# Four MetaFormer layers on one core: the wide stages' down products as three 64-column products, their eviction as a copy

## The chip, the cores and the metric

One core of one Trainium2 chip runs the whole program in one launch. The metric is the device time in microseconds (us), given as the median of several runs. TensorE's clock has two levels in the records, 1.2 and 2.4 GHz; the granted clock is given as a share of the upper one.

## The reference, cut to what matters

Sixteen images of 64 channels and 24 x 24 pixels go through four layers. Each layer normalizes, applies a small convolution-like mixer (a covariance gate, dynamic ReLU, a Haar gate, a 3x3 depthwise convolution), normalizes again and runs a mixture of eight experts on the 9216 tokens. Layers 0 and 1 run every expert on every token. Layers 2 and 3, the wide stages, send each token to its two best experts and compute

```python
h = silu(x @ w1[e].T) * (x @ w3[e].T)     # 64 -> 682
y = h @ w2[e].T                           # 682 -> 64
```

weighted by the router. The kernel computes in float16 pairs: a number is split into a high and a low half, and the three products high x high, high x low and low x high are added in float32. For the down projection, h is the pair in the tile `hl` (high half first, low half behind it), and w2 is the pair in the tiles `dW`, where each expert has 64 high columns and then 64 low columns.

## The kernel before, in words

The five engines each have one long, unrolled stream of instructions; semaphores tie them. A wide stage (`moe`) works on 80 tiles of 256 token rows, sorted by expert, in 20 rounds of four tiles (UNROLL). A tile belongs to one expert, known only at run time, so each expert's weights are addressed through a register of TensorE: `words`, `chosen` and `bases` (L1817 to L1830) decode the expert's number and multiply it by the width of one expert's columns.

A tile has three groups g. For each group TensorE runs, in this order written out by hand in `body23` (L1866):

- `up23` (L1832): eight products of 256 columns, gate and up, each for two blocks c of 114 hidden units and for the high and the low half of the weights (L1843 and L1844). Every one of these takes its weight block from another tile (gA, gB, uA, uB) at the offset in the register.
- `down23` (L1849) of the tile before: for each of two blocks c and two blocks u of 128 tokens, one product of the high half of h with 128 columns of weights, the 64 high and 64 low ones (L1860), and one of the low half of h with the 64 high columns (L1862). So a group has eight products, a tile 24, and the two stages 1920 of each line. The results for one u lie in 128 columns of an output bank: columns 0 to 63 hold high x high plus low x high, columns 64 to 127 hold high x low.

Once for each tile there are also two transposes of the next rows (`turn_rows`, L1814) and the decoding of the next expert (`settle`, L1823, called from L1846).

ScalarE takes the gate through Silu (L885) and rounds h to its high half (L893). VectorE multiplies (L1391), makes the low half (L1395) and, once for each tile, two tiles behind TensorE, adds the two 64-column halves out of the bank into the output row buffer (`evict`, L1372, the reduction at L1381). GpSimd then scatters each row buffer to memory (L675). The output banks are PB[4] and PB[5], used in turn.

The first two layers (`dense`) have a down step (L1785) that already runs three products of 64 columns into one place, from weights at a fixed address.

Of the kernel before, what the change touches and what calls it, by code (L numbers as in the profile page):

```python
# [21 lines left out]
ALU = mybir.AluOpType  # L22
ACT = mybir.ActivationFunctionType
AX = mybir.AxisListType
ds = bass.ds

B, C, HW = 16, 64, 24
PIX = HW * HW
P = 128
# [8 lines left out]
SUB = ROWS // P  # L38
# [16 lines left out]
CH = 114  # L55
# [171 lines left out]
def program(nc, I, out):  # L227
    ctx = ExitStack()
    with ctx:
        def sb(name, shape, dt=FP32):  # L230
            return ctx.enter_context(nc.sbuf_tensor(name, shape, dt))

        def sem(name):
            return ctx.enter_context(nc.semaphore(name))
# [79 lines left out]
        hl = [sb(f"hl{i}", [P, 4 * ROWS], FP16) for i in range(SPLIT)]  # L314
# [20 lines left out]
        PB = [ctx.enter_context(nc.psum_tensor(f"bank{i}", [P, 512], FP32)) for i in range(8)]  # L335
# [31 lines left out]
        s = {n: sem(n) for n in names}  # L367
# [23 lines left out]
        def group_base(l):  # L391

            return (l - SPARSE) * TILES * G

        def unit_base(l, h):
            return n_of(l, h) * NUNIT
# [29 lines left out]
        def tile_base(l):  # L426
            return (l - SPARSE) * TILES

        def ring(t):

            return t % YRING, 16 * SUB * (t // YRING)
# [10 lines left out]
        def inner():  # L442

            todo, begin, over = [LN1 + k / 4 for k in range(8)], JOIN_AT * G, JOIN_OVER * G
            return [-1] * begin + [todo[min(len(todo), -(-(v + 1) * len(todo) // over)) - 1] for v in range(NSLOT - begin)]
# [3 lines left out]
        def split_base(l):  # L449

            return (l - SPARSE) * TILES * SPLIT

        def hold(k, g):

            return prod[g]

        def wait_from(eng, semaphore, value):

            if not isinstance(value, int) or value > 0:
                eng.wait_ge(semaphore, value)  # L460
# [492 lines left out]
        def _(v):  # L953
# [414 lines left out]
            def moe(l, aside):  # L1368
                tb, gb = tile_base(l), group_base(l)
                plan = inner()  # L1370

                def evict(i, k):  # L1372

                    t = i * UNROLL + (tb + k)
                    v.wait_ge(s["y_grp"], i * (UNROLL * G) + (gb + (k + 1) * G))

                    r, before = ring(t)
                    wait_from(v, y_st[r], before)
                    y = ysb[r][:, :].rearrange("p (u c) -> p u c", u=SUB)
                    src = PB[4 + k % 2][:, 0:SUB * 2 * C].rearrange("p (u s c) -> p u c s", u=SUB, s=2)  # L1380
                    ins = v.tensor_reduce(y, src, AX.X, ALU.add)  # L1381
                    ins.then_inc(s["y_done"], 1)

                sb_ = split_base(l)

                def product(i, k, g):
                    q = k * G + g
                    p = hold(k, g)[0:CH, :]
                    v.wait_ge(s["s_ready"], i * (UNROLL * G) + (gb + q + 1))
                    v.wait_ge(s["h_ps"], i * (UNROLL * G) + (gb + q + 1))  # L1390
                    v.tensor_tensor(p, PB[2 + q % 2][0:CH, :], p, ALU.mult).then_inc(s["prod_ready"], 1)  # L1391

                def low(i, k, g):
                    v.wait_ge(s["hi_ready"], i * (UNROLL * SPLIT) + (sb_ + k * SPLIT + g + 1))
                    v.tensor_tensor(hl[g][0:CH, 2 * ROWS:4 * ROWS], hold(k, g)[0:CH, :], hl[g][0:CH, 0:2 * ROWS], ALU.subtract  # L1395
                                    ).then_inc(s["hp_ready"], 1)

                def body23(i, first=False):

                    for k in range(UNROLL):  # L1400
                        for g in range(G):
                            product(i, k, g)
                            if g > 0:
                                low(i, k, g - 1)
                            elif k > 0:
                                low(i, k - 1, G - 1)
                            elif not first:
                                low(i - 1, UNROLL - 1, G - 1)
                            if g == 0 and k >= 2:
                                evict(i, k - 2)  # L1410
                            elif g == 0 and not first:
                                evict(i - 1, k + UNROLL - 2)
                            if aside is not None:
                                aside.upto(plan[(i * UNROLL + k) * G + g])
                if l == SPARSE:
                    v.wait_ge(s["added"], unit_base(SPARSE, 0))
                body23(0, first=True)
                for i in range(1, LOOPS - 1):
                    body23(i)
                body23(LOOPS - 1)  # L1420
                low(LOOPS - 1, UNROLL - 1, G - 1)
                evict(LOOPS - 1, UNROLL - 2)
                evict(LOOPS - 1, UNROLL - 1)
                if aside is not None:
                    aside.upto(LAST)
# [111 lines left out]
        def _(pe):  # L1537
# [264 lines left out]
            def moe(l):  # L1802
# [46 lines left out]
                def down23(i, k, g):  # L1849


                    pe.wait_ge(s["hp_ready"], i * (UNROLL * SPLIT) + (split_base(l) + k * SPLIT + g + 1))
                    y = PB[4 + k % 2]
                    at = ds(bases[i * UNROLL + k, 1], 2 * C)
                    for c in range(2):
                        w = dW[2 * g + c][:, at]
                        for u in range(SUB):
                            col = c * ROWS + u * P
                            o = u * 2 * C
                            pe.matmul(y[:, o:o + 2 * C], hl[g][0:CH, col:col + P], w,  # L1860
                                      start=(g == 0 and c == 0 and u == 0), stop=False, skip_group_check=True)
                            ins = pe.matmul(y[:, o:o + C], hl[g][0:CH, 2 * ROWS + col:2 * ROWS + col + P],  # L1862
                                            w[:, 0:C], start=False, stop=(g == G - 1 and c == 1), skip_group_check=True)
                    ins.then_inc(s["y_grp"], 1)

                def body23(i, first=False, last=False):  # L1866

                    for k in range(UNROLL):
                        if not (last and k + 2 >= UNROLL):
                            turn_rows(i, k, 2)  # L1870
                        for g in range(g_):
                            up23(i, k, g, not (last and k == UNROLL - 1))
                            if k > 0:
                                down23(i, k - 1, g)
                            elif not first:
                                down23(i - 1, UNROLL - 1, g)
                            if g == 0 and k == 2 and not last:
                                fetch(i + 1)
                    if last:
                        for g in range(g_):  # L1880
                            down23(i, UNROLL - 1, g)
# [68 lines left out]
```

## Time and profile before

| | us |
|---|---|
| median of 3 runs | 2027.19 (2026.78 to 2030.93) |
| profiled execution, its own time | 2032.62 |
| span of the profile, first to last instruction | 2030.8 |
| mean granted clock of TensorE in the span | 0.826 |

The profile gives, for one execution, each engine's instructions with start and duration. PE is TensorE's products, PEld its weight loads, which overlap the products; PEldq is what TensorE's own instruction queue executes beside them (register arithmetic, semaphore waits), and these are not counted as busy. A product's duration includes its way through the array, so the distance from one start to the next says what it costs in a row of products. An idle time put down to "issue" is one in which the engine waited for nothing that the profile shows.

### The profile page before, as it was taken

Reading aid. Unit: us, or ns where it says so; the run is one execution under the profiler, and the core shown is the slowest. Engines: PE = TensorE matmul, PEld = TensorE weight load, DVE = VectorE, ACT = ScalarE, POOL = GpSimd, SP = SyncE. Lnnn points to the kernel's source line nnn. Section 1 sums busy time; section 2 is a strip of 40 time slices with the busy share of each in tenths; the row PEclk is TensorE's granted clock in tenths of the full one; section 3 lists DMA queues with packets and bytes.
Section 4 is the critical chain, followed back from the end, with each engine's and each line's share of the span. In section 5 each row is a group of like instructions: output and inputs, shape, how many; then the busy total and the mean of one; then the engine's idle time right before and its main releaser. Section 6 shows DMA issues by size and latency. Waiting matters only on the chain.

```text
span 2030.8 us, 47407 instructions
## 1 busy us (share of the span) xinstructions
PE 1452.7 (72%) x16020; PEld 1087.5 (54%) x16020; DVE 1687.7 (83%) x2922; ACT 1281.8 (63%) x2367; POOL 938.8 (46%) x899
## 2 busy tenths in 40 slices
PE   3648899526777776688349999995331449999994
PEld 2545444515333343344248888884221248888884
DVE  5676888697778858888669999999868769999998
ACT  1026899212999967499228888886320138888883
POOL 1003778100233311167027777656216757777653
PEclk9756999575999967699559999997655669999997
DMA  8000000000000100000001111210300011111212
GB/s 324 1 0 29 2 29 2 0 0 0 29 29 29 57 1 1 1 22 27 8 15 42 42 41 42 81 32 8 130 0 18 22 32 43 42 41 41 79 33 99
DMA packets 49470, 74.98 MB, mean 37 GB/s; under 512 B 13636, under 2 KB 34235, under 8 KB 46590
## 3 DMA queue, kind: packets, MB, share of 16 engines
q1 hardware_dynamic: 28354, 42.26, 6.5%
q0 software_dynamic: 20896, 29.73, 4.3%
q8 instruction: 146, 2.39, 0.5%
q14 instruction: 74, 0.61, 0.1%
HBM read 39.88 MB, written 33.08 MB: 36 GB/s over the span
## 4 chain that ended last, share of the span: by engine, by line
PE 37%; DVE 17%; issue 4%; ACT 2%; DMA 0%; POOLq 0%; POOL 0%; DVEq 0%; SPq 0%; ACTq 0%
PE bank L1843 13%; PE bank L1844 11%; PE bank L1860 5%; PE bank L1862 3%; DVE tmp L1181 2%; DVE x L1483 2%; PE bank L1715 1%; PE bank L1564 1%; PE bank L1814 1%; DVE xn L1003 1%; DVE st L1001 1%; DVE tmp L1154 1%; ACT hl L868 1%; DVE xn L1022 1%; DVE st L1002 1%
## 5 line engine op out<-in xcount | busy, mean ns | idle before, releaser
L689 POOL TENSOR_TENSOR x<-x,ysb 128x256 f32<-128x256 f32 x248 | 232.8, 939 | 620.9 <-DVE ysb L1489 603.6
L636 POOL DMA_INDIRECT rows<-rowsb,pos x288 | 306.7, 1065 | 205.7 <-DVE pos L1310 119.2
L868 ACT ACTIVATE hb<-bank,bias_sb 128x512 f32<-128x512 f32 x432 | 315.2, 730 | 85.0 <-issue 42.0
L675 POOL DMA_INDIRECT y<-w,ids x256 | 283.8, 1109 | 136.2 <-DVE w L1381 71.5
L1843 PE MATMUL bank<-xT,uA_ 128*114 128x256 f16 x960 | 258.0, 285 | 5.3
L1843 PE MATMUL bank<-xT,gA_ 128*114 128x256 f16 x960 | 251.2, 286 | 5.9 <-issue 3.6
L1844 PE MATMUL bank<-xT,uB_ 128*114 128x256 f16 x960 | 253.3, 278 | 0.0
L1391 DVE TENSOR_TENSOR act<-bank,act 114x512 f32<-114x512 f32 x320 | 219.8, 687 | 36.0 <-PE bank L1844 16.6
L885 ACT ACTIVATE act<-bank 114x512 f32<-114x512 f32 x320 | 191.2, 597 | 81.6 <-PE bank L1844 67.2
L1844 PE MATMUL bank<-xT,gB_ 128*114 128x256 f16 x960 | 242.3, 275 | 0.0
L1860 PE MATMUL bank<-dW_,hl 114*128 x1920 | 229.1, 220 | 3.1 <-DVE hl L1395 3.1
L1395 DVE TENSOR_TENSOR hl<-act,hl 114x512 f16<-114x512 f32 x320 | 218.3, 682 | 0.0
L1862 PE MATMUL bank<-dW_,hl 114*128 x1920 | 214.4, 192 | 0.0
L1472 DVE TENSOR_TENSOR hl<-hb,hl 128x512 f16<-128x512 f32 x216 | 165.6, 766 | 49.2 <-ACT hl L868 39.9
L1472 DVE TENSOR_TENSOR act<-hb,act 128x512 f16<-128x512 f32 x216 | 164.4, 761 | 43.8 <-ACT act L868 34.0
L893 ACT ACTIVATE hl<-act 114x512 f16<-114x512 f32 x320 | 199.1, 622 | 1.9 <-DVE act L1391 1.7
L1769 PE MATMUL bank<-rowsb,w 128*128 128x512 f16 x432 | 177.3, 410 | 4.2 <-DMA land<-land 3.5
L1770 PE MATMUL bank<-rowsb,w 128*128 128x512 f16 x432 | 177.2, 410 | 0.0
L1564 PE MATMUL bank<-K,xn 128*128 128x128 f32 x144 | 38.1, 409 | 193.2 <-DVE xn L1022 169.2
L1860 PEld LDWEIGHTS bank<-dW_,hl 114*128 114x128 f16 x1920 | 170.3, 97 | 7.1 <-issue 4.5
L1862 PEld LDWEIGHTS bank<-dW_,hl 114*128 114x128 f16 x1920 | 170.2, 98 | 0.0
L868 ACT ACTIVATE act<-bank,bias_sb 128x512 f16<-128x512 f32 x216 | 158.1, 732 | 0.0
(389 smaller groups left out, 3461.8 us busy)
## 6 DMA issues: line engine op xcount, KB each, us to landing
stage<-up SPq DMA_DIRECT2D x8, 1368.0 KB, 7.1
xs<-rows SPq DMA_DIRECT2D x160, 65.0 KB
rows<-land POOLq DMA_DIRECT2D x8, 1137.5 KB, 16.7
rows<-rowsb,pos POOLq DMA_INDIRECT x288
y<-w,ids POOLq DMA_INDIRECT x256, 2.3
stage<-down SPq DMA_DIRECT2D x2, 1368.0 KB
rowsb<-y SPq DMA_DIRECT2D x4, 640.0 KB, 6.2
x<-tokens SPq DMA_DIRECT2D x2, 1152.0 KB, 7.1
```

The source lines that it names most:

```text
L636: pool.indirect_dma_start(rows_d[l - SPARSE], bass.IndirectOffsetOnAxis(pos[h][:, k, j:j + 1], 0), words(h)[:, j * RW // 2:(j + 1) * RW // ...
L675: pool.indirect_dma_start(y_d, bass.IndirectOffsetOnAxis(ids[:, t * SUB + u:t * SUB + u + 1], 0), ysb[r][:, u * C:(u + 1) * C], None, boun ...
L689: pool.tensor_tensor(xv, xv, tg[u % 2], ALU.add).then_inc(s["added"], 1)
L868: ins = a.activation(dst[:, 0:SPAN * P], PB[w % 3][:, :], ACT.Gelu, scale=1.0 / WSCALE, bias=b1T[l][:, at:at + 1])
L893: a.activation(hl[g][0:CH, 0:2 * ROWS], hold(k, g)[0:CH, :], ACT.Copy).then_inc(s["hi_ready"], 1)
L1391: v.tensor_tensor(p, PB[2 + q % 2][0:CH, :], p, ALU.mult).then_inc(s["prod_ready"], 1)
L1395: v.tensor_tensor(hl[g][0:CH, 2 * ROWS:4 * ROWS], hold(k, g)[0:CH, :], hl[g][0:CH, 0:2 * ROWS], ALU.subtract).then_inc(s["hp_ready"], 1)
L1472: v.tensor_tensor(p[:, SPAN * P:2 * SPAN * P], hid[w % 2][:, 0:SPAN * P], p[:, 0:SPAN * P], ALU.subtract).then_inc(s["lo_ready"], 1)
L1843: pe.matmul(PB[bank][0:CH, o], w[0][2 * g + c][:, at], xT[k][:, :], start=True, stop=False)
L1844: ins = pe.matmul(PB[bank][0:CH, o], w[1][2 * g + c][:, at], xT[k][:, :], start=False, stop=True)
L1860: pe.matmul(y[:, o:o + 2 * C], hl[g][0:CH, col:col + P], w, start=(g == 0 and c == 0 and u == 0), stop=False, skip_group_check=True)
L1862: ins = pe.matmul(y[:, o:o + C], hl[g][0:CH, 2 * ROWS + col:2 * ROWS + col + P], w[:, 0:C], start=False, stop=(g == G - 1 and c == 1), ski ...
```

## The change: three products of 64 columns, and a copy

The product of 128 columns at L1860 becomes two of 64 columns, both with the high half of h as the loaded operand: one with the high and one with the low columns of the weights. All three products of a block now add into the same 64 columns, so an output bank holds 128 columns instead of 256, and the eviction is a copy of 128 columns instead of a sum over pairs of 128.

```diff
@@ def evict(i, k)
-                    src = PB[4 + k % 2][:, 0:SUB * 2 * C].rearrange("p (u s c) -> p u c s", u=SUB, s=2)
-                    ins = v.tensor_reduce(y, src, AX.X, ALU.add)
+                    src = PB[4 + k % 2][:, 0:SUB * C].rearrange("p (u c) -> p u c", u=SUB)
+                    ins = v.tensor_copy(y, src)
                     ins.then_inc(s["y_done"], 1)
@@ def down23(i, k, g)
                         w = dW[2 * g + c][:, at]
                         for u in range(SUB):
                             col = c * ROWS + u * P
-                            o = u * 2 * C
-                            pe.matmul(y[:, o:o + 2 * C], hl[g][0:CH, col:col + P], w,
+                            o = u * C
+                            pe.matmul(y[:, o:o + C], hl[g][0:CH, col:col + P], w[:, 0:C],
                                       start=(g == 0 and c == 0 and u == 0), stop=False, skip_group_check=True)
+                            pe.matmul(y[:, o:o + C], hl[g][0:CH, col:col + P], w[:, C:2 * C],
+                                      start=False, stop=False, skip_group_check=True)
                             ins = pe.matmul(y[:, o:o + C], hl[g][0:CH, 2 * ROWS + col:2 * ROWS + col + P],
                                             w[:, 0:C], start=False, stop=(g == G - 1 and c == 1), skip_group_check=True)
```

## Rows read from the trace of the kernel before

**Rows 1.** The page: span and count of instructions.

```profile
span 2030.8 us, 47407 instructions
```

**Rows 2.** Windows, the two wide stages: busy PE, PEld, DVE, ACT, POOL (count), clock, DMA, GB/s.

```profile
1050.00:1390.00 340.00, 331.12 (x3903) 300.03 (x3903) 319.58 (x549) 292.14 (x631) 243.23 (x224) 0.99 0.16 45
1668.00:2005.00 337.00, 329.66 (x3917) 297.38 (x3915) 323.59 (x553) 290.41 (x622) 235.15 (x218) 1.00 0.16 44
```

**Rows 3.** Waits, 1670 to 2005 us: PEld, PE, DVE (us in total, times, longest).

```profile
PEld bank L1843 <- issue: 25.1, 100, 0.4
...
PE bank L1860 <- DVE hl L1395: 1.7, 3, 0.8
...
DVE act L1391 <- ACT act L885: 4.0, 21, 0.2
```

**Rows 4.** Evictions by line L1381, second wide stage: ns min/median/max, first and last start.

```profile
L1381 DVE TENSOR_REDUCE w<-bank x64: 414/418/425, 1687.3 to 2005.1; 128x128 f32<-128x256 f32 x64
L1381 DVE TENSOR_REDUCE ysb<-bank x16: 411/418/420, 1670.1 to 1940.1; 128x128 f32<-128x256 f32 x16
```

**Rows 5.** Operations of TensorE's queue by line, 1750 to 1800 us (columns as before).

```profile
L1843 PEldq ALU_OP  x105: 32/32/32, 1750.1 to 1799.0; - x105
...
L1843 PEldq FUSED_REGOPS  x11: 42/42/42, 1753.1 to 1796.0; - x11
...
L1844 PEldq ALU_OP  x140: 32/32/36, 1750.3 to 1799.6; - x140
...
L1860 PEldq ALU_OP  x59: 32/32/32, 1751.4 to 1799.8; - x59
L1860 PEldq FUSED_REGOPS  x11: 42/42/42, 1754.0 to 1796.9; - x11
...
L1830 PEldq ALU_OP  x24: 36/36/36, 1750.8 to 1797.9; - x24
L1830 PEldq FUSED_REGOPS  x24: 90/90/90, 1751.0 to 1799.4; - x24
```

**Rows 6.** Timeline of TensorE's weight loads (start, duration, idle before).

```profile
1762.07 0.13 PEld L1843 LDWEIGHTS bank<-xT,gA_ 128*114 x1
...
1762.63 0.13 PEld L1844 LDWEIGHTS bank<-xT,uB_ 128*114 x1
...
1768.25 0.13 PEld L1843 LDWEIGHTS bank<-xT,uA_ 128*114 x1 [0.26 <-issue]
```

**Rows 7.** Timeline of TensorE's products in one group (start, duration).

```profile
1767.05 0.22 PE L1860 MATMUL bank<-dW_,hl 114*128 x1
...
1767.30 0.22 PE L1860 MATMUL bank<-dW_,hl 114*128 x1
...
1767.52 0.27 PE L1844 MATMUL bank<-xT,gB_ 128*114 128x256 f16 x1
...
1767.96 0.27 PE L1844 MATMUL bank<-xT,uB_ 128*114 128x256 f16 x1
```

**Rows 8.** Operations of the queue for the down products, the whole run.

```profile
L1860 PEldq ALU_OP  x800: 32/32/32, 1059.8 to 2004.3; - x160
L1860 PEldq FUSED_REGOPS  x160: 37/42/42, 1059.7 to 2002.2; - x160
```

**Rows 9.** Timeline of TensorE in the dense layer 1: one down step, and what follows.

```profile
519.71 0.51 PE L1785 MATMUL bank<-w1d,hl 128*128 128x64 f16 x12
520.06 0.38 PE L1769 MATMUL bank<-rowsb,w 128*128 128x512 f16 x1
```

**Rows 10.** Groups of VectorE by shape: copies out of a bank (busy us, mean ns).

```profile
L1154 DVE COPY tmp<-bank 128x512 f32<-128x512 f32 x32 | 22.0, 688 | 13.7 <-PE bank L1564 13.1
...
L1154 DVE COPY tmp<-bank 128x256 f32<-128x256 f32 x8 | 3.4, 420 | 3.9 <-PE bank L1564 3.9
```

**Rows 11.** Windows in the dense layer 1 (columns as in rows 2).

```profile
700.00:750.00 50.00, 35.91 (x344) 22.42 (x343) 31.50 (x48) 32.51 (x50) 8.79 (x11) 0.73 0.15 57
...
880.00:920.00 40.00, 35.34 (x506) 17.54 (x502) 35.73 (x106) 40.00 (x70) 31.16 (x31) 1.00 0.09 26
```

## The prediction

> **What bounds the kernel now.** First the windows of the two wide stages, since the change lies only there [rows 2]: 677 us of the 2030.8 us span [rows 1], at full clock. PE looks busy for 97 to 98% of them and VectorE for 94 to 96%; either could be the bound, and the change takes from VectorE and adds instructions to TensorE. So next the waits of the second stage [rows 3]. VectorE stood waiting 4.0 us for ScalarE, TensorE's products 1.7 us for VectorE: neither waits for the other. The largest entry is TensorE's weight loads, 25.1 us in 100 places, with "issue" as the cause: nothing outside TensorE made it wait. What is left is its own instruction queue.
>
> The pace: 80 evictions from 1670.1 to 2005.1 us [rows 4] are 79 steps of 4.24 us a tile. The array needs less. Starts of 256-column products lie 0.11 us apart (0.44 us over four), those of a pair L1860 and L1862 0.083 us (0.25 us over three) [rows 7]. A tile is 24 x 0.11 + 12 x 0.083, with some 0.1 us for two transposes 3.7 us: half a microsecond to spare. "98% busy" is the length of overlapping products.
>
> The queue has nothing to spare. Every product whose weights lie at a register address needs that address computed before it: an ALU_OP in the queue for each. In 50 us the lines L1843, L1844, L1860 and L1830 have 105 + 11 + 140 + 59 + 11 + 24 + 24 = 374 register operations [rows 5]; L1844 has 12 a tile, so this is 11.7 tiles and 32 operations a tile. An operation lasts 32 ns, but that isn't its price: 374 in 50 us is 134 ns each (semaphore waits and the fetch of the expert word included), and where the array is not behind, the loads follow one operation each at (1762.63 - 1762.07) / 5 = 112 ns [rows 6]. 32 x 112 ns is 3.6 us, and the waits, the fetch and the slow operations at L1830 make up the rest of 4.24. At 1768.25 the array is seen starving 0.26 us for the queue, behind the operations of L1830 [rows 6].
>
> **The change part by part.**
>
> *The second address.* L1860 has 960 queue operations in the run, 800 ALU_OP and 160 fused ones [rows 8], for 1920 products: 6 a tile, one for each block (g, c). Both u share it, and L1862, which begins at the same column, has none. After the change, two of the three products of a block begin at column 0 of the expert, and the third at column 64, so they need two different addresses. L1843 and L1844 show what a different constant costs: gA and gB are read at the same register offset and differ only in where the tile lies, and each product has an operation of its own [rows 5]. So I expect one more ALU_OP for each block, shared by both u: 6 a tile, 960 in all. At 112 ns that is 107 us, at the mean of 134 ns 129 us; at its duration of 32 ns 31 us. I take 115 ns, near the row where operations follow one another with products between them, as the new ones will: **+110 us**. Nothing hides it, since no engine is later than the queue: a tile goes from 4.24 to about 4.93 us.
>
> *The products.* 1920 products of 128 columns become 3840 of 64. The dense layer has the same thing, twelve products of 64 columns three by three into one place, from fixed addresses: the next product starts 0.35 us after the first of them [rows 9], 29 ns each. Three cost 88 ns where a pair costs 83: 5 ns x 1920 = 9 us of array time. The array has half a microsecond a tile to spare and needs 0.06 of it: **0**. If that cover were gone (no new operations, array the bound), +9 us. The 1920 added weight loads lie inside the 29 ns, as they do in the dense step. Twelve more products and loads pass through the queue a tile; a block of eight such instructions now adds nothing visible to its operation's 112 ns, so 0 up to the 9 us already named.
>
> *The eviction.* 160 reductions over 256 columns at 0.417 us [rows 4] become copies of 128. The trace has copies out of a bank of 512 columns, 688 ns, and of 256, 420 ns [rows 10]: 1.05 ns a column, so about 286 ns for 128, a gain of 0.13 us each, 21 us of VectorE's time. The bounds are 0 (a copy of 256) and 0.2 us. VectorE is not what a tile waits for, and waits more when TensorE slows: **0**. Only the very last eviction of a stage lies on the path, 0.1 us each.
>
> *Nothing else moves.* No wait and no DMA is added; the down products still end with one signal on the last of eight, now twelve. Queued behind the new ALU_OP are the next up products, for which ScalarE's Silu and VectorE's multiply wait, so both will idle more. GpSimd's two scatters a tile get more room.
>
> **Sum.** The profiled execution took 2032.6 us around its span of 2030.8; 110 more gives 2142.6. It lies 5.4 us above the median of 2027.2, to which I add the same: **2137 us**, 5.4% slower. The main case's high end is 129 us, 2156. For its low end, the queue's mean lies (134 - 112) x 32 = 0.7 us a tile above 112 ns an operation; most of that (semaphore waits, the fetch) is fixed, but if a quarter shrinks once the other engines have more room, 0.18 x 160 = 28 us come off the 107: 2106.
>
> **Rivals.**
>
> 1. *The queue needs no new operation* (not slower): the offset of 64 columns is carried by the product itself. For it: L1862 has no operation of its own. Against: it begins where L1860 begins, so that says nothing of another place, and the constants of gA and gB do cost an operation each. It decides by a count: 960 operations for the down products or 1920. Then the queue stays at 32 a tile and the array at 3.8 us: 2027, no change, up to +9 us. Chance 0.08.
>
> 2. *VectorE is the bound after all* and gives its gain back tile by tile: 160 x 0.13 = 21 us, 2006, if the queue needs nothing new. Its 96% speak for it; that the products wait 1.7 us for it, and the loads 25 us for the queue, against. 0.03.
>
> 3. *The operation costs its duration*, because the queue runs ahead in the down group, where two operations feed eight products (0.33 us of array time): 31 us, 2058. Against: over a tile the queue is what is late, and a lead gained in the down group is spent in the up group now. 0.04.
>
> 4. *Each added weight load is paid in full*: 1920 x 0.13 us, the duration of a load [rows 6], is 250 us, 2277. Against: twelve loads and products in 0.35 us in the dense step [rows 9]. 0.02. The Trainium skill speaks for this rival, in "TensorE: Matmul & The Clock Gate", section "Back-to-back issue gap": in a real stream of load and matmul pairs the spacing is set by both, about 81 ns at 128 columns. By that rule, taken for the 64-column products too, 36 products would need 2.9 us a tile and the array 5.7, an estimate of some 2260; but the pair would need 162 ns already now, and rows 7 show 83.
>
> 5. *The clock falls*, because products come at a slower rate. In the dense layer it is 0.73 where 344 products ran in 50 us, and 1.00 where 506 ran in 40 us and PE was idle for a tenth of the time [rows 11]. A wide stage will have 62 products a tile, over 600 in 50 us, 24 of each 62 with 256 columns. At the lower level, 1.2 GHz, the array's 3.8 us a tile doubles to 7.6, +2.7 us above 4.93; in a quarter of the tiles that is another 107 us, 2245. 0.02.
>
> 6. *The address is computed anew at each change of place*, for both u: two to four operations a block more than I count, 12 to 24 a tile more, 215 to 430 us more, 2350 or above. Against: the shared address at both u now. 0.01.
>
> The main case has the rest, 0.80.
>
> **How the numbers follow.** A measurement of this kernel can tell about 0.2%, 4 us, from no change. Slower by more: main case and rivals 3 to 6, 0.89. Within it: rival 1 but for a rest, 0.07. Faster: rival 2 and that rest, 0.04. The main case alone holds 8 in 10, so the range is its own, 2106 to 2156, widened for the 4 us by which the runs shown spread: 2102 to 2160.
>
> **What would show it.** Right: L1860 and the new line together have 1920 queue operations; the step of evictions is about 4.9 us and L1381's copies last about 0.29 us; weight loads wait longer for "issue", at the down products too; ScalarE and VectorE idle more, their busy time in a wide stage falls to some 80%; the starts of down products are no longer 29 ns apart but bunched behind the operations; the clock stays at 1.00. Wrong: 960 operations for the down lines, a step that stays at 4.2 us, or a stage in which the clock falls.

## The result, and the profile after

The changed kernel takes 2143.4 us, the median of 4 runs (2142.28 to 2145.31), where the kernel before took 2027.0 in 4 runs beside it (2026.01 to 2030.93). The ratio is 1.056, 95% interval 1.0537 to 1.0584. By this ratio the change costs 113.5 us, between 109 and 118; the two medians lie 116.4 us apart. The profiled execution took 2143.48 us around a span of 2141.7, against 2032.62 before: 110.9 us more.

First the page's span, with its count of instructions, of the changed kernel, to be set against [rows 1]:

```profile
span 2141.7 us, 52207 instructions
```

The added time lies in the wide stages. Their windows, in the columns of [rows 2]:

```profile
1050.00:1450.00 400.00, 388.93 (x4915) 338.70 (x4914) 323.98 (x556) 295.63 (x636) 253.67 (x224) 1.00 0.14 38
1728.00:2120.00 392.00, 376.90 (x4801) 326.85 (x4799) 321.67 (x549) 286.01 (x613) 249.19 (x217) 1.00 0.14 37
```

The second stage is 392 us where it was 337, at the same full clock, and VectorE, ScalarE and GpSimd do about the same work in it; of a longer window VectorE is busy for 82% where it was 96%, ScalarE for 73% where it was 86%. PE is still "busy" for 96%. That number, read alone, would call both kernels bound by the array.

The evictions and the queue of the changed kernel, by source line (in this kernel L1860 is high half by high columns, L1862 the new product of high half by low columns, L1864 low half by high columns); ns min/median/max, then the first and the last start:

```profile
L1381 DVE COPY w<-bank x64: 277/284/292, 1744.6 to 2116.0; 128x128 f32<-128x128 f32 x64
L1381 DVE COPY ysb<-bank x16: 277/284/288, 1724.6 to 2041.3; 128x128 f32<-128x128 f32 x16
...
L1860 PEldq ALU_OP  x800: 32/32/32, 1055.3 to 2115.5; - x160
L1860 PEldq FUSED_REGOPS  x160: 37/42/42, 1055.0 to 2113.1; - x160
...
L1862 PEldq ALU_OP  x800: 32/32/32, 1055.4 to 2115.6; - x160
L1862 PEldq FUSED_REGOPS  x160: 51/51/51, 1055.1 to 2113.3; - x160
```

L1862 has 960 operations of its own where the line had none before, beside the 960 that L1860 had [rows 8]; L1864 has none. The 80 evictions of the second stage span 2116.0 - 1724.6 = 391.4 us, 79 steps of 4.95 us; before it was 4.24 [rows 4]. That is 0.71 us a tile for six new operations, 119 ns each, and 160 x 0.71 = 114 us for both stages: the whole difference. The eviction itself fell from 0.418 to 0.284 us.

How the queue holds the products up is seen in one group, in the timeline of PE (start, duration):

```profile
1830.70 0.19 PE L1860 MATMUL bank<-dW_,hl 114*128 x1
1830.79 0.19 PE L1862 MATMUL bank<-dW_,hl 114*128 x1
1830.81 0.19 PE L1864 MATMUL bank<-dW_,hl 114*128 x1
1830.84 0.19 PE L1860 MATMUL bank<-dW_,hl 114*128 x1
1830.87 0.19 PE L1862 MATMUL bank<-dW_,hl 114*128 x1
1830.90 0.19 PE L1864 MATMUL bank<-dW_,hl 114*128 x1
1830.93 0.19 PE L1860 MATMUL bank<-dW_,hl 114*128 x1
1831.07 0.19 PE L1862 MATMUL bank<-dW_,hl 114*128 x1
...
1831.18 0.19 PE L1864 MATMUL bank<-dW_,hl 114*128 x1
1831.21 0.30 PE L1843 MATMUL bank<-xT,gA_ 128*114 128x256 f16 x1
```

The starts are 0.02 to 0.03 us apart, but for two: the first L1862 of each block c comes 0.09 and 0.14 us after the L1860 ahead of it. Those are the two places where the added address is first used. The twelve products take 0.51 us to the start of the next group's first up product. The group is typical: the second stage's trace holds 236 groups with all twelve products, and in 235 of them these same two starts lie more than 0.05 us behind the one before (a third one does in 10). On average such a group takes 0.53 us.

Who waits now, 1730 to 2115 us, by engine (us in total, times, longest):

```profile
PEld bank L1843 <- issue: 28.1, 107, 0.4
PEld bank L1862 <- issue: 1.3, 8, 0.2
...
DVE act L1391 <- ACT act L885: 30.4, 71, 0.5
DVE act L1391 <- PE bank L1844: 17.3, 49, 0.6
```

VectorE waited 4.0 us for ScalarE's gate before [rows 3], now 30.4; its wait for TensorE itself went from 1.7 to 17.3 us. The engines behind TensorE have more room. The row that named the queue, on the other hand, went from 25.1 to 28.1 only. The view lists a wait where the weight loads pause, and a load lasts 0.10 to 0.13 us, so most of a gap that an operation opens lies under the duration of the load before. The two loads at the second gap of the group above show it (start, duration):

```profile
1830.90 0.10 PEld L1860 LDWEIGHTS bank<-dW_,hl 114*128 114x128 f16 x1
1831.04 0.10 PEld L1862 LDWEIGHTS bank<-dW_,hl 114*128 114x128 f16 x1
```

The starts lie 0.14 us apart, of which 0.04 us are left as a pause, and the timeline marks no idle time there. The step of the evictions shows the price, the waits show only whom to suspect.

### The profile page after: what moved, and what is told of

Its sections match the earlier page's. It is cut to its first block, busy times and chain, and to the rows that moved or that the text cites. A ratio compares the mean times of both kernels' runs of the same rounds, so it can differ in the third digit from the quotient of the medians.

```text
span 2141.7 us, 52207 instructions
## 1 busy us (share of the span) xinstructions
PE 1551.3 (72%) x17940; PEld 1151.5 (54%) x17940; DVE 1684.5 (79%) x2922; ACT 1279.8 (60%) x2367; POOL 965.4 (45%) x899
## 4 chain that ended last, share of the span: by engine, by line
PE 40%; DVE 16%; issue 4%; ACT 3%; DMA 0%; POOLq 0%; POOL 0%; DVEq 0%; SPq 0%; ACTq 0%
PE bank L1843 14%; PE bank L1844 10%; PE bank L1862 6%; PE bank L1860 3%; PE bank L1864 3%; DVE tmp L1181 2%; DVE x L1483 2%; PE bank L1715 1%; PE bank L1564 1%; PE bank L1814 1%; DVE xn L1003 1%; DVE st L1001 1%; DVE tmp L1154 1%; ACT hl L868 1%; ACT act L868 1%
## 5 line engine op out<-in xcount | busy, mean ns | idle before, releaser
L636 POOL DMA_INDIRECT rows<-rowsb,pos x288 | 320.0, 1111 | 205.8 <-DVE pos L1310 119.3
L675 POOL DMA_INDIRECT y<-w,ids x256 | 291.3, 1138 | 213.1 <-DVE w L1381 154.6
L1860 PE MATMUL bank<-dW_,hl 114*128 x1920 | 284.0, 193 | 1.4 <-DVE hl L1395 1.2
L1843 PE MATMUL bank<-xT,uA_ 128*114 128x256 f16 x960 | 268.4, 289 | 13.7 <-issue 1.8
L1843 PE MATMUL bank<-xT,gA_ 128*114 128x256 f16 x960 | 254.5, 289 | 6.8 <-issue 6.4
L1844 PE MATMUL bank<-xT,uB_ 128*114 128x256 f16 x960 | 258.8, 277 | 0.0
L1862 PE MATMUL bank<-dW_,hl 114*128 x1920 | 247.1, 192 | 1.0
L1864 PE MATMUL bank<-dW_,hl 114*128 x1920 | 246.1, 192 | 0.0
L1862 PEld LDWEIGHTS bank<-dW_,hl 114*128 114x128 f16 x1920 | 175.9, 96 | 18.7 <-issue 2.0
L1860 PEld LDWEIGHTS bank<-dW_,hl 114*128 114x128 f16 x1920 | 180.4, 96 | 7.6 <-issue 2.4
```

Source lines behind the costliest of these rows:

```text
L636: pool.indirect_dma_start(rows_d[l - SPARSE], bass.IndirectOffsetOnAxis(pos[h][:, k, j:j + 1], 0), words(h)[:, j * RW // 2:(j + 1) * RW // ...
L675: pool.indirect_dma_start(y_d, bass.IndirectOffsetOnAxis(ids[:, t * SUB + u:t * SUB + u + 1], 0), ysb[r][:, u * C:(u + 1) * C], None, boun ...
L1843: pe.matmul(PB[bank][0:CH, o], w[0][2 * g + c][:, at], xT[k][:, :], start=True, stop=False)
L1844: ins = pe.matmul(PB[bank][0:CH, o], w[1][2 * g + c][:, at], xT[k][:, :], start=False, stop=True)
L1860: pe.matmul(y[:, o:o + C], hl[g][0:CH, col:col + P], w[:, 0:C], start=(g == 0 and c == 0 and u == 0), stop=False, skip_group_check=True)
L1862: pe.matmul(y[:, o:o + C], hl[g][0:CH, col:col + P], w[:, C:2 * C], start=False, stop=False, skip_group_check=True)
```

## Experiments

The theory was that TensorE's own queue sets the pace of a wide stage, and that each added address operation costs about 115 ns of it, whatever the products do. The first four runs were made together against the kernel before (2029.77 us there, the median of 19 runs, 2024.27 to 2038.73), the last four against 2031.74 (8 runs, 2025.07 to 2034.9).

**All of the change but the second address.** The changed kernel, its new product reading the first columns again:

```diff
-pe.matmul(y[:, o:o + C], hl[g][0:CH, col:col + P], w[:, C:2 * C],
+pe.matmul(y[:, o:o + C], hl[g][0:CH, col:col + P], w[:, 0:C],
```

> The changed kernel with the second product reading the high columns again instead of the low ones, so that all three products of a block use one address (it leaves out high h x low weights). As many products, loads and the same copy as the changed kernel, but 960 queue operations for the down lines, not 1920. Queue theory: the added time goes, 2027 to 2036 us (up to 9 us of array or fetch of the longer code). Rival, that the added products and weight loads (or three sums in a row into one place) cost it: it stays near 2143 us.

Measured: 2032.09 us (10 runs), ratio 1.0012 (0.9998 to 1.0026). Queue, evictions and products of this kernel, by source line and in PE's timeline:

```profile
L1860 PEldq ALU_OP  x800: 32/32/32, 1056.2 to 2003.4; - x160
L1860 PEldq FUSED_REGOPS  x160: 37/42/42, 1056.1 to 2001.3; - x160
...
L1381 DVE COPY w<-bank x64: 276/284/292, 1685.2 to 2003.9; 128x128 f32<-128x128 f32 x64
L1381 DVE COPY ysb<-bank x16: 283/284/286, 1668.0 to 1939.5; 128x128 f32<-128x128 f32 x16
...
1830.38 0.20 PE L1860 MATMUL bank<-dW_,hl 114*128 x1
1830.42 0.19 PE L1862 MATMUL bank<-dW_,hl 114*128 x1
1830.44 0.19 PE L1864 MATMUL bank<-dW_,hl 114*128 x1
...
1830.73 0.30 PE L1843 MATMUL bank<-xT,gA_ 128*114 128x256 f16 x1
```

L1862 has no operation of its own. With the same 17940 products and loads as the changed kernel, and the same copies, a tile takes (2003.9 - 1668.0) / 79 = 4.25 us, the pace of before. The twelve products take 0.35 us, with no gap, where the changed kernel took 0.51; on average over the stage it is 0.37 against 0.53. So 1920 more products, 1920 more loads and the short copy together are worth 2 us, with an interval of 0 to 5 (the copy's own share is found below); nearly all of the 113 belongs to the second place in the weights.

**The second address alone.** The kernel before, with its pair of products kept; the low half of h reads the low columns:

```diff
 ins = pe.matmul(y[:, o:o + C], hl[g][0:CH, 2 * ROWS + col:2 * ROWS + col + P],
-                w[:, 0:C], start=False, ...
+                w[:, C:2 * C], start=False, ...
```

> The kernel before with the product of the low half of h reading the low columns instead of the high ones (low h x low weights in place of low h x high weights), nothing else: the products, loads and the eviction of before, but a second address in each block, 1920 queue operations. Queue theory: 960 more operations at 112 to 125 ns, 2134 to 2147 us. Rival, that products or loads cost it: 2027 us.

Measured: 2139.5 us (4 runs), ratio 1.0558 (1.0529 to 1.0586). By source line:

```profile
L1862 PEldq ALU_OP  x800: 32/32/32, 1056.2 to 2112.8; - x160
L1862 PEldq FUSED_REGOPS  x160: 51/51/51, 1056.0 to 2110.5; - x160
...
L1381 DVE TENSOR_REDUCE w<-bank x64: 410/418/425, 1744.0 to 2113.2; 128x128 f32<-128x256 f32 x64
L1381 DVE TENSOR_REDUCE ysb<-bank x16: 417/418/418, 1724.0 to 2039.1; 128x128 f32<-128x256 f32 x16
```

The old products and the old eviction, and 960 operations more: (2113.2 - 1724.0) / 79 = 4.93 us a tile. By the ratios, 1.0558 and 1.056, the loss is that of the changed kernel. One offset in one product, in a kernel otherwise unchanged, costs 5.6%. Together with the run above this shows the operation as the cause from both sides: taken away the loss is gone, put in alone it is there.

**The copy alone.** The kernel before, evicting one of the two halves:

```diff
-src = PB[4 + k % 2][:, 0:SUB * 2 * C].rearrange("p (u s c) -> p u c s", u=SUB, s=2)
-ins = v.tensor_reduce(y, src, AX.X, ALU.add)
+src = PB[4 + k % 2][:, 0:SUB * 2 * C].rearrange("p (u s c) -> p u s c", u=SUB, s=2)[:, :, 0, :]
+ins = v.tensor_copy(y, src)
```

> The kernel before with its eviction made a copy of the 128 high columns (it leaves out the high x low part of the sum); TensorE's stream is that of before. Queue theory: VectorE is not what a tile waits for, 2025 to 2029 us, the copy 0.28 us instead of 0.42. Rival, VectorE as the bound: 160 x 0.13 us less, 2006 us.

Measured: 2028.05 us (10 runs), ratio 0.9987 (0.9962 to 1.0011). The evictions:

```profile
L1381 DVE COPY w<-bank x64: 283/284/291, 1683.8 to 2000.5; 128x128 f32<-128x128 f32 x64
L1381 DVE COPY ysb<-bank x16: 283/284/284, 1666.6 to 1936.4; 128x128 f32<-128x128 f32 x16
```

Each is 0.134 us shorter, 21 us in all. The kernel's time is 2 us shorter by the medians, and by the interval between 8 us shorter and 2 us longer: a tile takes 4.23 us. An engine that is busy for 95% of a stage gave back next to nothing when its work was cut.

**Three addresses.** A dose of twice the size: the low half's product reads at another column for each u.

```diff
-                w[:, 0:C], start=False, ...
+                w[:, C // (u + 1):C // (u + 1) + C], start=False, ...
```

> As the pair with two places, but the product of the low half of h reads at column 64 for the first block of tokens and at column 32 for the second, so a block needs three addresses (low h x other weights in place of low h x high weights): 1920 operations more than before, products and loads as before. Queue theory, linear in operations: +215 to +240 us, 2242 to 2267 us. If an operation only costs where the array leaves no cover, the second step is larger than the first; if the products cost, 2027 us.

Measured: 2253.36 us (4 runs), ratio 1.1125 (1.1096 to 1.1153). By source line, and the window of the second stage in the columns of [rows 2]:

```profile
L1862 PEldq ALU_OP  x1600: 32/32/32, 1055.7 to 2225.4; - x178
L1862 PEldq FUSED_REGOPS  x320: 46/51/51, 1055.3 to 2223.1; - x160
...
L1381 DVE TENSOR_REDUCE w<-bank x64: 410/418/425, 1802.4 to 2225.7; 128x128 f32<-128x256 f32 x64
L1381 DVE TENSOR_REDUCE ysb<-bank x16: 417/418/420, 1779.6 to 2140.6; 128x128 f32<-128x256 f32 x16
...
1780.00:2225.00 445.00, 430.53 (x3891) 363.00 (x3892) 331.29 (x548) 288.00 (x619) 218.98 (x215) 1.00 0.12 33
```

1920 operations more, (2225.7 - 1779.6) / 79 = 5.65 us a tile. From 0 to 960 to 1920 operations the medians go 2029.8, 2139.5, 2253.4: +109.7 and +113.9, a straight line at 116 ns an operation. By the ratios the steps are +113 and +115, 118 and 119 ns an operation. Had the queue had slack for some of them, the first dose would have been cheaper than the second by that slack; it is cheaper by 4 us (2 by the ratios), which the intervals hold. And PE is 97% "busy" in this window too, with the same number of products in a stage that has grown from 337 to 445 us: the row says that some product is always under way, not that the array is full.

**One wait less.** If the queue is the bound, taking anything out of it must pay. At the first group of a tile `up23` waits for a transposed tile although `turn_rows`, run just ahead of it, has already waited for a later count of the same semaphore. The kernel before without that second wait; the result is the same:

```diff
-def up23(i, k, g, ahead):
+def up23(i, k, g, ahead, turned_before):
...
-    if g == 0:
+    if g == 0 and not turned_before:
         pe.wait_ge(s["xT_done"], i * UNROLL + (tb + k + 1))
...
-up23(i, k, g, not (last and k == UNROLL - 1))
+up23(i, k, g, not (last and k == UNROLL - 1), not (last and k + 2 >= UNROLL))
```

> The kernel before without the second wait for the turned rows at the head of a tile: TensorE has waited for a later count of the same semaphore in the transposes just ahead, so the semaphore wait that stood alone in its queue goes (155 of some 318 in the wide stages; the result is unchanged). Products, addresses and evictions as before. Queue theory: the queue had 126 ns from this entry to the next, 155 x 0.11 to 0.126 us less, 2007 to 2010 us. Rival, that only register operations count or that the array or VectorE sets the pace: no change, 2027 us.

Measured: 2017.51 us (4 runs), ratio 0.9929 (0.9907 to 0.995). By source line (L460 is the helper through which waits are issued):

```profile
L460 PEldq EVENT_SEMAPHORE  x166: 51/51/51, 277.6 to 1983.0; - x166
```

There were 321 of these, so 155 are gone, and with them 14.2 us of 2031.74, 92 ns each (66 to 122 by the interval). Expected were 17 to 20: the gain is real, 10 to 19 by the interval, which overlaps with what was expected. By the medians its size was put a little too high. A wait for something long done isn't free in the engine that sets the pace.

**Decoding at the point of use.** The two base addresses of a tile are no longer computed ahead and kept; the multiplication stands where the address is used; the result is the same:

```diff
-bases[t, step - 1] = pe.snap(pe.to_reg(chosen[t] * n), min_val=0, max_val=(E - 1) * n)
+bases[t, step - 1] = chosen[t] * n
```

> The kernel before with the multiplication of the expert's number by the column width left to the place where the address is computed, so that the two fused operations of the decoding (168 ns from each to the next entry) go, an ordinary 112 ns operation stands in the place of each, and two other fused operations have one step more (result unchanged). Queue theory: 2 x 56 ns less, some 10 to 20 ns more, a tile: 13 to 16 us less, 2011 to 2016 us. If only the number of operations counted (it stays at 34 a tile): 2027 us.

Measured: 2020.4 us (5 runs), ratio 0.9942 (0.9914 to 0.997), 11.3 us less. By source line:

```profile
L1843 PEldq ALU_OP  x2080: 32/32/47, 1052.1 to 1985.9; - x190
L1843 PEldq FUSED_REGOPS  x160: 46/46/46, 1052.3 to 1982.8; - x160
```

L1830 is gone, with its 320 plain operations and 318 fused ones of 90 ns; L1843 has 636 plain ones more than the 1444 it had. So the count of operations is the same within two, and what went is the 318 long ones, in whose place stand short ones: 11.3 us over 318 is 36 ns each (19 to 55 by the interval), where the durations differ by 58. By the medians the gain is short of the 13 to 16 us that were expected; the interval, 6 to 17 us, holds them.

**Both.** The two edits together:

> Both of the two edits above together in the kernel before (result unchanged). Queue theory: the gains add up to some 0.2 us a tile, 1994 to 2000 us, unless VectorE, whose seven starts of a tile need some 3.96 us without any wait, becomes the bound on the way: then 2000 to 2006 us. Rival, pace not set by the queue: 2027 us.

Measured: 2005.6 us (4 runs), ratio 0.9876 (0.9855 to 0.9898), 26.1 us less than before, about the sum of the two (25.5). It misses the 1994 to 2000 that the queue theory gave and lies in the 2000 to 2006 that were said for VectorE as the bound on the way; the next run asks about that. Evictions, waits and window of its second stage:

```profile
L1381 DVE TENSOR_REDUCE w<-bank x64: 412/418/424, 1666.4 to 1972.0; 128x128 f32<-128x256 f32 x64
L1381 DVE TENSOR_REDUCE ysb<-bank x16: 417/418/418, 1650.1 to 1908.9; 128x128 f32<-128x256 f32 x16
...
PEld bank L1843 <- issue: 8.0, 41, 0.4
...
1650.00:1972.00 322.00, 317.84 (x3897) 298.65 (x3895) 317.04 (x550) 281.30 (x619) 229.28 (x216) 1.00 0.17 46
```

A tile takes (1972.0 - 1650.1) / 79 = 4.07 us, and the loads' wait for the queue is 8.0 us where it was 25.1 [rows 3]. This version computes all that the kernel before computes and is faster than both: by 1.2% than the one before, by 6.4% than the changed one (2005.6 against 2143.4).

**Both, and the copy.** With a shorter queue VectorE is busy for 98% of that window. If it had become the bound, the copy would be worth something now:

```diff
-ins = v.tensor_reduce(y, src, AX.X, ALU.add)
+ins = v.tensor_copy(y, src)
```

(with the copy's source as in the run of the copy alone, and the two edits of the run above).

> Both edits, and the eviction a copy of the 128 high columns (it leaves out the high x low part of the sum). It asks whether the shorter eviction is worth anything once the queue is shorter. Queue still the bound: as with both edits alone, within 3 us. VectorE the bound by then: up to 160 x 0.13 us = 21 us less than with both edits alone.

Measured: 2003.53 us (4 runs), ratio 0.9867 (0.9841 to 0.9894). The evictions:

```profile
L1381 DVE COPY w<-bank x64: 283/284/291, 1670.8 to 1975.9; 128x128 f32<-128x128 f32 x64
L1381 DVE COPY ysb<-bank x16: 277/284/285, 1654.4 to 1913.5; 128x128 f32<-128x128 f32 x16
```

2.1 us less than without the copy, with intervals that overlap almost wholly, and again (1975.9 - 1654.4) / 79 = 4.07 us a tile. At 98% busy VectorE is still not what a tile waits for. What is left of the bound at 4.07 us, the queue's 32 operations or the array's 3.7 us with the transposes, was not taken apart by a run. The traces lean to the queue. Counted from one eviction to the next, over the first 72 steps of the second stage, the queue has 34.3 entries a tile in the kernel before (register operations, semaphore waits, fetches of the expert word), 40.3 in the changed kernel, 46.2 in the double dose and 33.2 with both edits. The mean distance from one entry to the next is 125, 125, 124 and 124 ns. It hardly changes, and the step follows the number of entries.

## Why the prediction was right, point by point

The forecast was 2137 us, slower, in 2102 to 2160; 2143.4 came, by the mechanism that it named. Most of the 6 us between them is the 5.4 that the sum took off because the profiled execution of the kernel before lay that far above its median; that of the changed kernel, 2143.48, lay on its median.

*What bounds.* That the queue sets the pace, not the array and not VectorE, was the step on which all hung. Three runs bear it out, each from another side: operations added cost in proportion to their number, VectorE's work cut gave 2 us of 21 (0 to 8 by the interval), and waits and long operations taken out of the queue gave 26 us.

*The second address.* One new operation for each block, shared by both u, 960 in all: the count is exact, down to the split into 800 plain and 160 fused. The price was taken at 115 ns, between 112 and 134. It is 113.5 us / 960 = 118 ns by the ratio, 119 ns by the step of the evictions. With the address alone it is 114 by the step and by the medians and 118 by the ratio; in the double dose 116 by the medians, 117 by the step, 119 by the ratio. On the profiled executions, against which the sum was made, it came to 110.9 us for the 110 forecast. The row gave 112 and the mean 134; that the value chosen between them came so close is partly luck. The shrinking of waits by a quarter, from which the low end came, wasn't seen.

*The products and loads.* Put at 0, with 9 us if their cover were gone: 0 to 5 us with the copy beside them. The starts 0.03 us apart that were read from the dense layer [rows 9] hold here, 0.35 us for twelve.

*The eviction.* 286 ns was estimated, 284 measured; worth 0 was said, and 2 us were found for the copy alone and again with the queue shortened, with 0 inside the interval.

*Signs in the profile.* The count of 1920, the step (4.93 forecast, 4.95 measured), the copies and the clock of 1.00 came as stated. Three were looser. The loads' wait for "issue" grew by only 3 us in the view of waits at L1843, and by 1.3 us at L1862, as told above; the view was trusted to show more than it can. ScalarE went to 73%, VectorE to 82%, where "some 80%" stood for both: 86% and 96% times 4.24 / 4.95 would have given 74% and 82%. And the down products aren't bunched throughout; two starts of twelve wait, the rest follow at about 0.03 us.

*The rivals.* No new operation (2027): refuted by the count. VectorE as the bound (2006): by the copy alone. The bare duration (2058): 114 to 119 ns against 32, in three kernels. Address computed for each u (2350): by the count. The clock (2245): 1.00 in both windows. Loads paid in full (2277): by the first experiment, where 1920 more loads and products, with the shorter copy beside them, cost 2 us. The Trainium skill spoke for that rival, in "TensorE: Matmul & The Clock Gate", section "Back-to-back issue gap", with about 81 ns for a load and product of 128 columns; the runs don't agree for this stream: the pair of 128 and 64 columns, two loads and two products, takes 83 ns [rows 7], and products of 64 columns, each with its own load, follow at 0.35 us / 12 = 29 ns.

## What to carry to other kernels

Where an operand lies at a register address, count the distinct (register, constant) pairs, not the products: in this kernel each pair cost one operation a block in the engine's own queue, however many products of the block shared it. Where that queue sets the pace, reading a second place in a tile that is already addressed isn't free. Before trusting 97% busy, compare the steps at which the stage really advances with the distances between starts in an undisturbed row of the same instructions; what was left over here was time of the engine's own queue. And look in a queue that binds for waits that an earlier wait already covers and for long register operations; in this kernel two such edits of a line or two gave 1.2%, where the change cost 5.6%.

## What the runs showed that was not expected

- An address operation lasts 32 ns in the record and costs 114 to 119 ns of the queue. A semaphore wait of 51 ns cost 92. A fused register operation of 90 ns in place of a plain one of 32 cost some 36 ns more. So the price isn't the duration, nor a fixed multiple of it. It is close to the distance at which the queue's entries start one after another: in the wide stages of all ten traces the next entry starts a median of 113 ns after an address operation. After a wait it starts a median of 116 ns later in the kernel before, and after a fused operation of L1830 174. Why the entries keep this distance was not found.
- The weight loads and products themselves pass through the same queue almost for nothing: 1920 of each, with the shorter copy beside them, added 0 to 5 us. More instruction bytes aren't the price either: the first experiment fetched more of them than the double dose and ran 221 us faster. The page's row of instruction fetch (packets, MB, share) for these two kernels, in that order:

```profile
q8 instruction: 161, 2.64, 0.5%
```

```profile
q8 instruction: 154, 2.52, 0.4%
```

- The changed kernel's median lies 4 us above that of the address alone (2139.5), but the two were measured in different rounds. Against the kernel before in its own round the ratios are 1.056 and 1.0558, so the address accounts for the whole loss within the intervals.
